# A routed-expert kernel whose token blocks are ordered in phases, with the results read back inside the block loop

## What is computed

```python
x = x + rglru(layernorm(x))          # x: 4 x 512 x 256, a gated complex linear recurrence over 512 steps
x = x + moe(layernorm(x))            # 2048 tokens, width 256

def moe(x):                          # 32 experts in 8 groups, hidden width 128
    s = sigmoid(x @ gate_w.T)        # best 4 groups by their largest score, then best 6 experts in them
    c = 2.5 * s_top6 / sum(s_top6)
    y = sum over the 6 chosen e of c_e * (silu(x @ w11[e].T) * (x @ w33[e].T)) @ w22[e].T
    return y + (silu(x @ sw1.T) * (x @ sw3.T)) @ sw2.T    # shared expert, hidden width 256
```

## Time and profile before

| | |
|---|---|
| median of 3 runs | 489.14 us (488.16 to 490.08) |
| the profiled execution | 492.55 us, of which 490.1 us are the span of its instructions |
| PE busy | 406.6 us, 83% |
| DVE busy | 286.1 us, 58% |
| POOL busy | 229.4 us, 47% |
| ACT busy | 223.3 us, 46% |

### The profile page before, as it was taken

One profiled execution on the slowest core, in us unless ns is written; L12 is line 12 of the kernel. 1 busy time (PEld: TensorE's weight loads), 2 busy tenths in 40 slices (PEclk: granted clock), 3 DMA queues, 4 the chain that ended last, 5 costly groups with the idle time before them and its releaser, 6 DMA issues.

```text
span 490.1 us, 9413 instructions
## 1 busy us (share of the span) xinstructions
PE 406.6 (83%) x1804; PEld 306.6 (63%) x1805; DVE 286.1 (58%) x943; ACT 223.3 (46%) x587; POOL 229.4 (47%) x242
## 2 busy tenths in 40 slices
PE   3869678929777644486999999999999999997987
PEld 2535355726555411345888888888888888883576
DVE  3768779999888450011555555555555555552497
ACT  2778957675851400001445554554554554541011
POOL 1000003807787777771455565565565655563000
PEclk9888785865957759588999999999999999999899
DMA  7500000303249999834565555555555555404996
GB/s 256 232 0 2 0 1 30 119 13 121 109 156 424 420 385 346 304 127 122 170 191 162 167 167 158 171 161 166 169 161 162 171 165 168 131 14 146 423 417 214
DMA packets 42658, 86.03 MB, mean 176 GB/s; under 512 B 8197, under 2 KB 33549, under 8 KB 42128
## 3 DMA queue, kind: packets, MB, share of 16 engines
q1 hardware_dynamic: 28304, 53.85, 32.0%
q0 software_dynamic: 10752, 28.34, 16.9%
q10 hardware_dynamic: 3584, 3.64, 2.2%
HBM read 49.97 MB, written 40.01 MB: 184 GB/s over the span
## 4 chain that ended last, share of the span: by engine, by line
PE 54%; POOL 17%; DVE 12%; issue 7%; ACT 6%; DMA 3%; SPq 0%; DVEq 0%; POOLq 0%; ACTq 0%
PE PS L1142 23%; POOL bucket_rows L393 17%; PE PS L1156 12%; PE PS L1135 6%; PE PS L1149 3%; PE PS L1010 3%; PE PS L1105 3%; DMA resid<-in_x 2%; DVE expert_weights L287 2%; PE PS L1055 1%; DVE st L634 1%; PE PS L1112 1%; ACT L567 1%; DVE expert_weights L289 1%; DVE expert_weights L290 1%
## 5 line engine op out<-in xcount | busy, mean ns | idle before, releaser
L408 POOL DMA_INDIRECT choice_rows<-block_out_s,block_meta x128 | 125.9, 984 | 98.0 <-issue 70.1
L393 POOL DMA_INDIRECT bucket_rows<-payload,dest x96 | 101.1, 1053 | 117.9 <-DVE dest L828 89.9
L1142 PE MATMUL PS<-expert_weights,block_rows_t 128*128 x512 | 133.2, 383 | 0.0
L1142 PEld LDWEIGHTS PS<-expert_weights,block_rows_t 128*128 128x128 f32 x512 | 88.3, 192 | 6.9
L1156 PE MATMUL PS<-expert_weights,block_hidden_t 128*128 x256 | 78.0, 387 | 0.0
L587 ACT ACTIVATE block_rows_t<-PS 128x256 f32<-128x256 f32 x128 | 49.0, 383 | 53.8 <-PE PS L1135 53.3
L930 DVE SCALAR_TENSOR_TENSOR block_hidden_s<-block_silu_s,block_meta,PS 128x128 f32<-128x128 f32 x128 | 44.5, 348 | 45.5 <-ACT block_silu_s L577 43.9
L577 ACT ACTIVATE block_silu_s<-PS 128x128 f32<-128x128 f32 x128 | 35.5, 277 | 63.7 <-PE PS L1142 63.7
L924 DVE COPY block_meta<-block_rows_s 128x2 f32 x128 | 22.5, 176 | 57.4 <-issue 57.4
L936 DVE COPY block_out_s<-PS 128x256 f32<-128x256 f32 x128 | 53.7, 420 | 3.8 <-PE PS L1156 3.7
L1135 PE MATMUL PS<-ident,block_rows_s 128*128 128x128 f32 x256 | 49.2, 274 | 4.2 <-DMA block_rows_s<-bucket_rows 4.2
(11 more groups left out here) (184 smaller groups left out, 547.8 us busy)
## 6 DMA issues: line engine op xcount, KB each, us to landing
block_rows_s<-bucket_rows SPq DMA_DIRECT2D x128, 160.0 KB, 2.3
expert_weights<-choice_rows SPq DMA_DIRECT2D x16, 768.0 KB, 14.7
expert_weights<-in_experts SPq DMA_DIRECT2D x1, 4224.0 KB, 14.1
expert_weights<-in_experts SPq DMA_DIRECT2D x1, 3456.0 KB, 16.0
bucket_rows<-pad_rows SPq DMA_DIRECT2D x19, 160.0 KB
expert_weights<-in_experts SPq DMA_DIRECT2D x1, 2688.0 KB, 18.3
bucket_rows<-pad_rows ACTq DMA_DIRECT2D x14, 160.0 KB
resid<-in_x SPq DMA_DIRECT2D x4, 512.0 KB, 9.5
```

The costliest lines, as they stand in the source:

```text
L393: nc.gpsimd.indirect_dma_start(out=bucket_ap[:, :], out_offset=bass.IndirectOffsetOnAxis(ap=dest[:, t, k:k + 1], axis=0), in_=PAY[:, t, :] ...
L408: nc.gpsimd.indirect_dma_start(out=choice_ap[:, :], out_offset=bass.IndirectOffsetOnAxis(ap=meta_id[:, slot, 1:2], axis=0), in_=yy[:, slot ...
L1142: ins = mm(PS[:, 2 + r, 0:2 * P], xT[:, r, k * P:(k + 1) * P], W[:, bass.ds(w + k * 2 * P, 2 * P)], start=(k == 0), stop=(k == KD - 1))
```

## The change

- The blocks are ordered by token instead of by expert alone. There are five phases (ends of chunks 1 to 5, that is token tiles 4, 8, 12, 14 and 16). A block belongs to the first phase whose tokens open it, so that after a number of blocks known beforehand (`blocks_through`: 56, 79, 103, 115, 127) all rows of the phase's tokens are written. The table on DVE is worked out over 5*32 = 160 entries.
- There are 127 blocks. An expert's last block is moved back so that it ends with the bucket's last row, and shares rows with the one before it; the 33 paddings behind the buckets become one transfer of 32 tiles ahead of the buckets, issued at the start. Row numbers of `choice_rows` run backwards, and the bound of POOL's scatter falls when a phase is closed, so that rows already read back are not written again.
- The shared expert of all four batches runs ahead of the loop.
- Steps from 64 on are written out on SP, ACT, DVE and PE, and on POOL those from block 56 on. `Fori` keeps 7 passes (POOL 7 as well).
- In the written-out steps SP reads token tiles 0 to 11 back (`load_choices`, at the steps of `LOAD_AT`) into a ring of six tiles that lies where the payload and the transposed rows were. DVE adds one of the six rows at a time onto `resid` (`add_choice`), one per step for tiles 0 to 7 and two per step for tiles 8 to 11 (`ADD_AT`, `ADD_RATE`), and ACT stores the finished tile. Tiles 12 to 15 follow after the loop. PE sums no tile any more.

```diff
...
-    BLOCKS = N * TOPK // P + E
+    BLOCKS = (N * TOPK + E * (P - 1)) // P
...
+    PHASE_ENDS = (1, 2, 3, 4, 5)
+    PH = len(PHASE_ENDS)
+    V5 = PH * E
+    UNROLL_AT = 64
+    RING = 6
+    LOAD_AT = {0: 70, 1: 73, 2: 76, 3: 79, 4: 94, 5: 97, 6: 100, 7: 103, 8: 117, 9: 119, 10: 121, 11: 123}
+    ADD_AT = {0: 66, 1: 72, 2: 78, 3: 84, 4: 90, 5: 96, 6: 102, 7: 108, 8: 113, 9: 117, 10: 121, 11: 125}
+    ADD_RATE = {n: 1 if n < 8 else 2 for n in range(NT)}
...
+        RINGS = ROWS[:, 0:RING * TOPK * D].rearrange("p (s k d) -> p s k d", s=RING, k=TOPK)
...
-        def pad_buckets(eng, which):
-            for e in which:
-                row = eng.value_load(tabs[0:1, 3 * P + e:3 * P + e + 1], min_val=0, max_val=E * CAP)
-                eng.dma_start(bucket_ap[bass.ds(row, P), :], PADT[:]).then_inc(s_pad, 16)
...
+        def all_scattered(eng, bound):
+            for q in range(NY):
+                eng.wait_ge(s_ys[q], 16 * len(range(q, bound, NY)))
+        def phase_of(n):
+            return next(i for i, c in enumerate(PHASE_ENDS) if CHUNKS[c][0] * TS + CHUNKS[c][1] + CHUNKS[c][2] > n)
+        def blocks_through(phase):
+            b, t0, nt = CHUNKS[PHASE_ENDS[phase]]
+            bound = ((b * TS + t0 + nt) * P * TOPK + E * (P - 1)) // P
+            return -(-bound // NXS) * NXS if phase == 0 else bound
+        FIRST_BOUND = blocks_through(0)
+        def rows_open(j):
+            done = [i for i in range(PH) if blocks_through(i) <= j]
+            if not done:
+                return 1 + N * TOPK
+            b, t0, nt = CHUNKS[PHASE_ENDS[done[-1]]]
+            return 1 + (NT - b * TS - t0 - nt) * P * TOPK
...
-            sp.dma_start(bucket_ap[PADROW:PADROW + P, :], PADT[:]).then_inc(s_pad, 16)
+            sp.dma_start(bucket_ap.rearrange("(e c) r -> c e r", c=CAP)[0:P],
+                         PADT[:].unsqueeze(1).to_broadcast([P, E, ROW])).then_inc(s_pad, 16)
...
-            sp.wait_ge(s_padrow, 1)
-            pad_buckets(sp, range(ACT_PADS, E))
             sp.wait_ge(s_tab, 1)
-            sp.wait_ge(s_pad, 16 * (E + 1))
+            sp.wait_ge(s_pad, 16)
...
+            def load_choices(n):
+                all_scattered(sp, blocks_through(phase_of(n)))
+                if n < RING:
+                    sp.wait_ge(s_resid, B)
+                else:
+                    sp.wait_ge(s_fin, n - RING + 1)
+                sp.dma_start(RINGS[:, n % RING].rearrange("p k d -> p (k d)"), choice_t[NT - 1 - n]).then_inc(s_cin[n], 16)
...
-            with sp.Fori(NXS, BLOCKS, NXS) as i:
+            with sp.Fori(NXS, UNROLL_AT, NXS) as i:
                 for u in range(NXS):
                     load_block(i + u, u, i + (u - NXS + 1))
-            for q in range(NY):
-                sp.wait_ge(s_ys[q], 16 * (BLOCKS // NY))
+            for j in range(UNROLL_AT, BLOCKS):
+                load_block(j, j % NXS, j - NXS + 1)
+                for n in range(NT):
+                    if LOAD_AT.get(n) == j:
+                        load_choices(n)
             for n in range(NT):
-                sp.dma_start(flat[:, n * TOPK * D:(n + 1) * TOPK * D], choice_t[n]).then_inc(s_cin[n], 16)
+                if n not in LOAD_AT:
+                    load_choices(n)
             for n in range(NT):
-                if n not in PE_SUMS:
-                    sp.wait_ge(s_fin, dve_sums(n) + 1)
-                    sp.dma_start(out_d[n], resid[:, n, :]).then_inc(s_out[0], 16)
-            sp.wait_ge(s_out[0], 16 * dve_sums(NT))
+                if n not in LOAD_AT:
+                    sp.wait_ge(s_fin, n + 1)
+                    sp.dma_start(out_d[n], resid[:, n, :]).then_inc(s_out, 16)
+            sp.wait_ge(s_out, 16 * (NT - len(LOAD_AT)))
...
+            pool.reg_mov(end_row, rows_open(0) - 1)
+            with pool.Fori(0, FIRST_BOUND, NXS) as i:
                 for u in range(NXS):
-                    scatter(i + u, u, i + u + 1)
+                    scatter(i + u, u, i + u + 1, rows_open(0))
+            for j in range(FIRST_BOUND, BLOCKS):
+                if rows_open(j) != rows_open(j - 1):
+                    pool.reg_mov(end_row, rows_open(j) - 1)
+                scatter(j, j % NXS, j + 1, rows_open(j))
...
-            act.wait_ge(s_padt, 1)
-            act.wait_ge(s_padrow, 1)
-            pad_buckets(act, range(ACT_PADS))
-            for b in range(SHARED_BEFORE):
+            for b in range(B):
...
+            def store(n):
+                act.wait_ge(s_fin, n + 1)
+                act.dma_start(out_d[n], resid[:, n, :]).then_inc(s_out_act, 16)
             for s in range(NXS):
                 step(s, s)
-            with act.Fori(NXS, BLOCKS, NXS) as i:
+            with act.Fori(NXS, UNROLL_AT, NXS) as i:
                 for u in range(NXS):
                     step(i + u, u)
-            for s in range(BLOCKS, BLOCKS + 3):
+            stored = 0
+            for s in range(UNROLL_AT, BLOCKS + 3):
                 step(s, s)
-            for b in range(SHARED_BEFORE, B):
-                shared(b)
-            for q, n in enumerate(PE_SUMS):
-                act.wait_ge(s_sump, q + 1)
-                if q >= 2:
-                    act.wait_ge(s_out[1 + q % 2], 16 * (q // 2))
-                A(SUMMED[q % 2], PS[:, q % 2, 0:D], ACT.Copy).then_inc(s_fin_act, 1)
-                act.wait_ge(s_fin_act, q + 1)
-                act.dma_start(out_d[n], SUMMED[q % 2]).then_inc(s_out[1 + q % 2], 16)
-            act.wait_ge(s_out[1], 16 * ((len(PE_SUMS) + 1) // 2))
-            act.wait_ge(s_out[2], 16 * (len(PE_SUMS) // 2))
+                if stored in ADD_AT and ADD_AT[stored] + TOPK // ADD_RATE[stored] + 1 <= s:
+                    store(stored)
+                    stored += 1
+            for n in range(stored, len(LOAD_AT)):
+                store(n)
+            act.wait_ge(s_out_act, 16 * len(LOAD_AT))
...
+            dve.wait_ge(s_outp, NCH)
             c.wait()
-            V.tensor_copy(tabs[0:1, 3 * P:3 * P + E], cb[0:1, :]).then_inc(s_padrow, 1)
-            c.add(STT(cnti[:, 0, :], cb[:], float(P - 1), cb0[:], AD, SU))
+            c.add(STT(by_phase(BLK_I[0]), cbs[:, PHASE_ENDS[0] + 1:PHASE_ENDS[-1] + 2, :], float(P - 1), all_phases(cbs[:, 0, :]), AD, SU))
+            c.add(V.memset(UPTO[:, 0, :], 0.0))
+            c.add(V.memset(DONE[:, 0:1], 1.0))
+            dve.wait_ge(s_dve, c.n - 2)
+            c.add(TSC(BLK_I[1], BLK_I[0], 7, None, ALU.logical_shift_right))
+            c.add(TSC(by_phase(quant[:, 1, :]), all_phases(cbs[:, NCH, :]), -float(P), None, AD))
+            dve.wait_ge(s_dve, c.n - 1)
+            c.add(V.tensor_copy(UPTO[:, 1:, :], by_phase(BLK_I[1])))
             c.wait()
-            c.add(TSC(cnti[:, 1, :], cnti[:, 0, :], 7, None, ALU.logical_shift_right))
+            c.add(TT(by_phase(PER_V), UPTO[:, 1:, :], UPTO[:, 0:PH, :], SU))
             c.wait()
-            c.add(V.tensor_copy(cnt[:, CBK, :], cnti[:, 1, :]))
+            c.add(V.tensor_tensor_scan(CUM, PER_V, PER_V, 0.0, AD, ALU.bypass))
             c.wait()
-            c.add(V.tensor_tensor_scan(cnt[:, CUM, :], cnt[:, CBK, :], zero_e[:], 0.0, AD, AD))
+            c.add(TSC(DONE[:, 1:], CUM, iota_p[:, 0:1], None, ALU.is_le))
+            c.add(TT(by_phase(OPENED), UPTO[:, 1:, :], by_phase(CUM), SU))
             c.wait()
-            c.add(TSC(cnt[:, LE, :], cnt[:, CUM, :], iota_p[:, 0:1], None, ALU.is_le))
+            c.add(STT(by_phase(quant[:, 0, :]), by_phase(OPENED), float(P), all_phases(cbs[:, 0, :]), M, AD))
+            c.add(TT(PER_V, DONE[:, 0:V5], DONE[:, 1:], SU))
             c.wait()
-            c.add(TT(cnt[:, TMP, :], cnt[:, LE, :], cnt[:, CBK, :], M))
-            c.add(V.tensor_reduce(tabf[:, 0:1], cnt[:, LE, :], X, AD))
+            c.add(TT(PICKS, quant[:], PER_V.unsqueeze(1).to_broadcast([P, 3, V5]), M))
             c.wait()
-            c.add(V.tensor_reduce(tabf[:, 1:2], cnt[:, TMP, :], X, AD))
+            c.add(V.tensor_reduce(tabf[:, 0:3], PICKS, X, AD))
             c.wait()
-            c.add(TT(tabf[:, 1:2], iota_p[:], tabf[:, 1:2], SU))
-            c.wait()
-            c.add(TSC(tabf[:, 1:2], tabf[:, 1:2], float(P), None, M))
-            c.wait()
-            c.add(STT(tabf[:, 2:3], tabf[:, 0:1], float(CAP), tabf[:, 1:2], M, AD))
-            c.wait()
-            TSC(tabf[:, 2:3], tabf[:, 2:3], float(PADROW), None, ALU.min).then_inc(s_tabf, 1)
-            c.add(TSC(tabf[:, 3:4], tabf[:, 0:1], float(E - 1), float(EW), ALU.min, M))
-            c.add(TSC(tabf[:, 4:5], tabf[:, 0:1], float(E - 1), 2.0, ALU.min, M))
-            c.wait()
-            TSC(tabf[:, 4:5], tabf[:, 4:5], float(D), None, AD).then_inc(s_tabf, 1)
+            STT(tabf[:, 3:4], tabf[:, 0:1], j128[:, 0:1], tabf[:, 1:2], AD, ALU.min).then_inc(s_tabf, 1)
+            TSC(tabf[:, 4:5], tabf[:, 2:3], float(EW), None, M).then_inc(s_tabf, 1)
+            TSC(tabf[:, 5:6], tabf[:, 2:3], 2.0, float(D), M, AD).then_inc(s_tabf, 1)
...
+            adds = {"done": 0}
```

(52 more changed lines are left out.)

105 lines of the change are left out of this document (48 added, 57 removed).

## The result

The changed kernel takes **476.89 us** (median of 4 runs, 474.49 to 479.31) against 489.61 us for the kernel before in the same measurement (488.16 to 490.58): ratio 0.972, 95% interval 0.966 to 0.979. It is faster, and within the range of 464 to 482; the forecast was 471.6, so 5.3 us too low.

What follows compares the result with a forecast made beforehand. It took POOL's bucket scatters to bound the front, PE the loop and transfers the tail. Front +15.5, loop -3.1 and tail -30.0 gave -17.6 us, from 489.14 to 471.6 us, range 464 to 482.

Steps and rivals of the forecast that it cites:

- Front: Before the loop: longer table and all four batches of shared expert delay the first block product to 242.5, +15.5 us.
- Passages of the loop: In the loop: eight passages fewer from one pass to the next, 0.48 us each, -3.8 us.
- One addition a step: In the loop: one DVE addition of 0.42 us fits each of 48 steps, which keep 1.63 us.
- steps with two additions: In the loop: DVE needs about 1.93 us against 1.63 in each of 12 steps, +1.6 us (0 to 5).
- Read-backs: In the loop: each lands in about 5.7 us beside the loop's transfers, and is mostly hidden.
- late rows: In the loop: tiles 0, 4 and 8 wait 0.3 us each for their read-back, +0.8 us (0 to 9).
- rival "slower than before": In the loop: read-backs delay scatters, taken slots of `yy` hold DVE; 495 to some 509 us; chance 0.04.
- The sum of the loop: The loop from first product to last copy: -3.1 us in all, 213.4 us long.
- POOL's port: Loop and tail: rival that additions hold POOL's scatters and POOL sets the pace, about +8, 479.6 us; chance 0.14.
- the rival of 467.3: In the front: the clock holds through the shared expert, all second halves take 3.72 us; chance 0.11.
- Tail: After the last copy: 16.6 us instead of 46.55, -30.0 us.
- the 1 us for POOL: In the tail: 12 unbroken additions beside POOL's last two scatters, +1 us (0 to 4.8).

Runs made afterwards that it cites:

- e1: The kernel before with the shared expert of all four batches ahead of the loop, nothing else changed; ratio 1.065 to the kernel before.
- e1b: The kernel before with only the shared expert of all four batches moved ahead of the loop, run again on another chip; ratio 1.045.
- e2: The changed kernel without the read-backs of tiles 0 to 11, all additions kept; ratio 0.946 to the kernel before.
- e2b: The changed kernel without the read-backs of tiles 0 to 11, all additions kept, run again on another chip; ratio 0.941 to the kernel before.
- e5: The changed kernel with each batch's second half behind the next one's first half, and batch 0 started before the table's products; ratio 0.951 to the kernel before.
- e3: The changed kernel with all read-backs, but for tiles 0 to 11 one column added once instead of six rows; ratio 0.946 to the kernel before.
- r0: The changed kernel itself, run again on another chip; ratio 0.979 to the kernel before.

## Why the prediction was right, and which term was mis-sized

- **Front, right.** Table 4.9 us (forecast 5.0), first block 241.1 (242.5). The 1.4 between them are the second halves (mean 4.53 instead of 4.8, 1.1 in all) and the shared expert's start (182.1 instead of 182.7), and 0.16 us by which each of three batches starts before the end of the one ahead, less batch 0's first half (9.51 instead of 8.79), to rounding. The prediction did name the padding as the cause of the late silu and let it vanish at no cost. It had none in the new place either: the last `dest` ends at 175.8 us instead of 176.3. The gap that went, 10.6 us, is most of the 12.7 that the change gains.
- **Passages of the loop, mis-sized.** I took 0.48 us for each from one row. Of the 14 in the kernel before, two cost that (at 306.7 and 346.8), one 0.37 and the rest 0.25 to 0.29: 4.3 together. The changed kernel has six for 1.9. So 2.4 us come off, not 3.8. The 1.6 us of the first two steps, which the forecast did not have, make up for it by luck.
- **One addition a step, right.** Where no transfer is late, the written-out steps are 1.63 us with an addition in each: PE's `gate_up` starts at 373.11, 374.74 and 376.37. The additions take 424 ns each, as supposed. The first three steps with two additions (from 434.4) take 1.63 too. What the others cost (forecast +1.6 for all) can't be read: all long steps behind 434 us come behind a slot wait too, and sum to 2.6.
- **Read-backs, the step that failed.** The forecast put +0.8 for late rows and nothing for slots; a scatter lands in about 2.2 us, and its slot is wanted 3.1 us after that. The mechanism is that of my rival "slower than before", and the landing of 6.8 us at which it was to decide was passed by three of the five scatters in the chain (6.2 to 7.3). What I had wrong there is how often: it decided only if each of the 12 read-backs stalled DVE by 1.5 us. Ten waits came, three of them over 1.5, one of 1.04 and six under 1, and DVE's slack takes up to 0.6 of each before PE sees it. Slots and double additions together cost 7.9 us against a forecast of 1.6, late rows 0.9 against 0.8. The read-backs themselves landed in 5.1 to 7.7 us where the forecast had 5.7 (eight of the twelve took over 7).
- **The sum of the loop.** 216.5 - 1.6 (a block) - 2.4 (passages) - 1.6 (the first two steps take 1.18 and 1.19, since four blocks' rows are there; 2.07 and 1.89 before) + 8.8 + 0.8 (from the last `gate_up` to the last copy's end 4.6 us instead of 3.8) - 0.2 (first product to first `gate_up`) = 220.3; measured 220.7.
- **POOL's port, not borne out.** POOL's scatters before took 982/983/996 ns (least, median, most). The changed kernel's, by tile:

```profile
L435 POOL DMA_INDIRECT choice_rows<-block_out_s,block_meta x127: 982/983/1197, 247.3 to 463.4; - x127
```

The written-out half has 66 for 65.8 us busy, the half without additions 59 for 58.05: 13 ns more each, 0.9 us in all. The Trainium skill's rule (SBUF — State Buffer, "SBUF: two separate sides"), by which an addition would block a scatter for its whole length or be blocked by one, is not what these traces show for additions of 0.42 us: of the 53 scatters of the unrolled part that overlap an addition eight are over 1.00 us, and none is lengthened by more than 0.22. The longest addition took 0.50. For DVE instructions that follow each other without a gap this says nothing: the 2.49 us of the earlier trace rows stand beside seven of them, in the recurrence.
- **Clock.** 5.41 us in the last second half, 0.90 mean over the shared expert: the rival of 467.3 did not come: two of the four second halves took 3.72.
- **Tail, right.** 15.8 us against 16.6. The scatter landed in 2.08 and the last tile's wait was 2.98; the 1 us for POOL was not needed. One reading behind it does not hold: the row of the tail before has PE busy 15.00 us and DVE 14.56 of 15, so it does not show the transfers alone as the limit there.
- **Not the change: POOL's long stop.** POOL once stood 4.24 us ahead of block 113's scatter (443.36), not far from a phase's end, at which its register is set. The kernel before has the same stop at the same block, and has no phases:

```profile
425.73 0.98 POOL L408 DMA_INDIRECT choice_rows<-block_out_s,block_meta  x1 [3.32 <-DVE block_out_s L936]
```

All traces with four slots have it: 3.3 us in e1 and e1b, 3.2 in e2, e2b and e5, 3.5 in e3, 4.0 in r0. So neither the phases nor the read-backs make it. What does is open, and so is how much it adds to the slot waits behind it.

## What to carry to other kernels

Work moved into a loop brings its transfers along, and a transfer that hides its own latency can still lengthen that of small ones on the same engines: count the buffers of every producer by the landing time that they will have then, not by the one that they have now. When a wait is taken away, see which wait stands next in line; here eight slots alone showed no gain, and the gain came with the later additions. And when a step is moved, look for what was queued ahead of it in the old place: the padding in ACT's queue had held PE for 10.6 us, against 13 for each batch that was moved.

## What the runs showed of the hardware

A scatter of 128 rows lands in 2.6 us (median) in the changed kernel with no plain transfer of 768 KB in flight, and in 5.2 with one, at most 7.3; the DMA share of that half is 0.77 in the mean.

A passage of the hardware loop costs PE 0.25 to 0.33 us, in 4 of 20 passages 0.37 to 0.49, though its eight steps are the same instructions each time.

Chips differ. On three others the kernel before took 54 to 60 us more, and the changed one 57 on the one chip where it ran; in it 29 us of that were lost before the shared expert started, in waits such as this of r0, for which the trace names no releaser on the core:

```profile
DVE dpos L846 <- remote: 16.7, 1, 16.7
```

What it is was not tried. Ratios carry over only roughly: 0.972 on one chip and 0.979 on another for the same two kernels.
